# Graph layer and mixture of experts on one core: 36 weight chunks turned by transposing transfers instead of by the matrix engine

## The reference, cut to what matters

```
def gnn(x, C, A):                      # called with C = A = adj, 2048 x 2048
    S = (A + A.T) * 0.5 + eye          # degrees of S give dinv
    y = C @ (dinv[:, None] * S * dinv[None, :])
    return y @ x
def bit_quant(W):                      # per row of W
    scale = clip(mean(abs(W), -1), 1e-5, None)
    return clip(round(W / scale), -1, 1) * scale
def ffn(h):                            # 1 shared expert, 8 routed ones, top 1
    shared = silu(h @ sw1.T) @ sw2.T
    routed = gate * (silu(h @ ew1[e].T) @ ew2[e].T)   # e = best expert of the token
    return shared + routed
x = x + gnn(layernorm(x), adj, adj)    # x is 2048 x 512
x = x + ffn(layernorm(layernorm(x) * gamma + beta))
```

## Time and profile before

| | |
|---|---|
| median of three runs | 680.46 us (679.86 to 681.08) |
| profiled execution, first to last instruction (span) | 677.9 us |
| PE busy | 628.0 us, 93% |
| DVE, ACT, POOL busy | 69%, 55%, 26% |
| SP's transfer queue (q1) | 57.8% of 16 DMA engines, over the whole span |
| granted TensorE clock, mean | 0.997 |

### The profile page before, as it was taken

The page is one execution under the profiler, slowest core; times in us unless marked ns, Lnnn a source line. Parts: engine busy times, 40 slices in busy tenths (PEclk is TensorE's granted clock), DMA queues, the critical chain, the costliest instruction groups (busy, mean ns, idle before and its releaser), DMA issues.

```text
span 677.9 us, 15256 instructions
## 1 busy us (share of the span) xinstructions
PE 628.0 (93%) x4993; PEld 364.5 (54%) x4993; DVE 470.1 (69%) x1035; ACT 374.6 (55%) x692; POOL 178.2 (26%) x205
## 2 busy tenths in 40 slices
PE   0789899999987999999988999999999999999995
PEld 0334344444433444444434477776776777767772
DVE  4878997777775555678879399878865655555553
ACT  1667646668795777687746224566543333233331
POOL 2234443232210000003325244000122544353422
PEclk9999999999999999999999999999999999999998
DMA  8999980985768787767676967994395897777641
GB/s 348 418 421 414 421 335 2 221 208 158 227 198 293 258 281 270 266 225 237 210 256 233 226 181 179 232 232 127 73 191 153 191 195 184 184 173 196 168 137 32
DMA packets 107551, 151.67 MB, mean 224 GB/s; under 512 B 64734, under 2 KB 64734, under 8 KB 103392
## 3 DMA queue, kind: packets, MB, share of 16 engines
q1 hardware_dynamic: 91728, 117.74, 57.8%
q0 software_dynamic: 6960, 20.99, 10.3%
q10 hardware_dynamic: 8800, 12.09, 6.4%
HBM read 119.57 MB, written 19.16 MB: 205 GB/s over the span
## 4 chain that ended last, share of the span: by engine, by line
PE 56%; issue 28%; DVE 6%; DMA 6%; POOL 3%; ACT 0%; POOLq 0%; DVEq 0%; SPq 0%; ACTq 0%
PE bank L1625 20%; PE bank L1653 19%; DMA region<-in_adj_t 6%; PE bank L1502 5%; PE bank L1504 5%; PE bank L1503 5%; DVE region L1085 2%; DVE region L1081 1%; POOL rb L691 1%; POOL hb L698 1%; DVE region L1109 1%; DVE work L1105 1%; PE bank L1638 0%; DVE work L1340 0%; DVE work L1350 0%
## 5 line engine op out<-in xcount | busy, mean ns | idle before, releaser
L1653 PE MATMUL bank<-region,work 128*128 (+1 forms) x624 | 141.2, 379 | 1.9 <-DVE work L1350 1.9
L965 ACT ACTIVATE work<-work 128x512 f32<-128x512 f32 x78 | 48.5, 621 | 146.9 <-DVE work L1340 142.5
L1502 PE MATMUL bank<-zreg,work 128*128 (+1 forms) x256 | 97.2, 380 | 10.4 <-DVE work L1271 7.2
L1625 PE MATMUL bank<-zreg,region 128*128 128x128 f16 x1728 | 100.9, 219 | 0.0
L1625 PEld LDWEIGHTS bank<-zreg,region 128*128 (+1 forms) x1728 | 98.2, 98 | 4.5
L1502 PE MATMUL bank<-region,work 128*128 128x512 f16 x192 | 74.0, 385 | 25.7 <-DVE region L1109 25.5
L1504 PE MATMUL bank<-zreg,work 128*128 (+1 forms) x256 | 97.0, 379 | 0.0
L1503 PE MATMUL bank<-zreg,work 128*128 (+1 forms) x256 | 97.0, 379 | 0.0
L1653 PEld LDWEIGHTS bank<-region,work 128*128 128x128 f16 x624 | 59.1, 98 | 67.1 <-issue 4.4
L835 ACT ACTIVATE junk<-work 128x512 f16<-128x512 f32 x116 | 72.8, 627 | 24.6 <-DMA work<-in_w 18.3
L1350 DVE SCALAR_TENSOR_TENSOR work<-work 128x512 f16<-128x512 f32 x78 | 53.4, 691 | 38.8 <-ACT work L972 38.5
(11 more groups left out here) (163 smaller groups left out, 914.0 us busy)
## 6 DMA issues: line engine op xcount, KB each, us to landing
work<-in_w SPq DMA_DIRECT2D x58, 512.0 KB, 4.3
region<-in_adj SPq DMA_DIRECT2D x16, 1024.0 KB, 10.7
region<-in_adj_t SPq DMA_DIRECT2D x16, 1024.0 KB, 7.6
work<-in_adj_t SPq DMA_DIRECT2D x32, 384.0 KB, 4.4
zreg<-s_scratch SPq DMA_DIRECT2D x24, 256.0 KB, 4.0
xb<-in_w SPq DMA_DIRECT2D x10, 512.0 KB, 4.3
zreg<-in_x SPq DMA_DIRECT2D x4, 1024.0 KB, 9.8
h_scratch<-hb POOLq DMA_DIRECT2D x16, 256.0 KB, 4.3
```

The lines of the kernel that those rows point to most:

```text
L965: nc.scalar.activation(h1[:, cols], pre[:, cols], ACT.Silu).then_inc(h1_ok, 1)
L1502: nc.tensor.matmul(dst, a_hi, b_hi, start=start, stop=False, skip_group_check=True)
L1625: last = nc.tensor.matmul(ps_h[b][f // 4][:, (f % 4) * P:(f % 4 + 1) * P], w, ht[n % RING][:, c:c + P], start=(f % 4 == 0 and d == 0 and h ...
L1653: last = nc.tensor.matmul(ps_y[b][:, :].rearrange("p (d c) -> p d c", d=DB), h1hl[:, b, h, f * P:(f + 1) * P], w, start=(f == 0 and h == 0 ...
```

## The change

`by_dma` becomes true for every chunk but the eight early ones of even number that PE turns. SP gets `turn_later`, called two steps after the chunk's own step, right behind that step's `load_w`; PE's `turn_w` loses all its calls in the second product; ACT's `store_w` and DVE's `ternary` wait on `turned[...]` of the chunk's step instead of `tr_ok`. In macro 0 SP waits for the end of the first product (`z_acc`) before the first of these transfers, as their destination holds data of that product until then. Two loops are partly written out.

```
         def by_dma(q):
-            return isinstance(q, int) and (q >= LATE_FROM or q < ALL_BY_DMA or q < EARLY_CHUNKS and q % 2 == 1)
+            return not (isinstance(q, int) and ALL_BY_DMA <= q < EARLY_CHUNKS and q % 2 == 0)
...
+            def turn_later(g, m, s):
+                q, kind, c = later(g, m, s)
+                dst = (w1t if kind == 1 else w2t)[:, ds(c * CHUNK, CHUNK)]
+                sp.wait_ge(tern_ok, q + 1)
+                sp.dma_start(dst[:, WORDS:CHUNK].bitcast(I16).rearrange("p (k r) -> p k r", r=P),
+                             words16[:, s, :], transpose=True).then_inc(turned[s], 16)
...
                     if not weight_free(m):
                         load_w(later(g, m - (g == 2), s), s % 2)
+                    if s >= 2 and not weight_free(m):
+                        if isinstance(m, int) and m == 0 and s == 2:
+                            sp.wait_ge(z_acc, NT)
+                        turn_later(g, m - (g == 2), s - 2)
+                    elif s < 2 and not (isinstance(m, int) and (m == 0 or weight_free(m - 1))):
+                        turn_later(g, m - 1 - (g == 2 and m - 1 > IDLE), s + 2)
...
                 if by_dma(q):
-                    act.wait_ge(*turned_by(q))
+                    act.wait_ge(*turned_by(q, step))
                     nc.scalar.activation(values, dst[:, WORDS:CHUNK].bitcast(I8).rearrange("p (w b) -> p b w", b=2),
                                          ACT.Sign).then_inc(wt_ok, 1)
...
                     if by_dma(before_q):
-                        dve.wait_ge(*turned_by(before_q))
+                        dve.wait_ge(*turned_by(before_q, step))
...
                 for s in range(STEPS):
                     b = s % 2
-                    late_turn = first and g == 1 and s == 1
-                    idle = isinstance(m, int) and m == IDLE
-                    if s and not (late_turn or weight_free(m)):
-                        turn_w(later(g, m - (g == 2), s - 1), s - 1)
-                    elif s == 0 and isinstance(m, int) and m == 0:
-                        turn_w(early(ROUNDS - 1, early_count(ROUNDS - 1) - 1), 3)
-                    elif s == 0 and not (isinstance(m, int) and weight_free(m - 1)):
-                        turn_w(later(g, m - 1 - (g == 2 and not idle), STEPS - 1), STEPS - 1)
                     pe.wait_ge(atlo_ok, STEPS * m + s + 1)
```

More of the change, by code:

```diff
@@ L364, in by_dma, with turned_by @@
         def by_dma(q):
-            return isinstance(q, int) and (q >= LATE_FROM or q < ALL_BY_DMA or q < EARLY_CHUNKS and q % 2 == 1)
+            return not (isinstance(q, int) and ALL_BY_DMA <= q < EARLY_CHUNKS and q % 2 == 0)
         def nth_by_dma(q):
             return q if q < ALL_BY_DMA else ALL_BY_DMA + (q - ALL_BY_DMA) // 2
-        def turned_by(q):
-            if q < EARLY_CHUNKS:
+        def turned_by(q, step=None):
+            if isinstance(q, int) and q < EARLY_CHUNKS:
                 d = nth_by_dma(q)
                 return turned[d % 4], 16 * (d // 4) + 16
-            return late_turned[q % 2], 16 * ((q - LATE_FROM) // 2) + 16
+            if isinstance(q, int) and q >= LATE_FROM:
+                return late_turned[q % 2], 16 * ((q - LATE_FROM) // 2) + 16
+            s = q % STEPS if isinstance(q, int) else step
+            return turned[s], 16 // STEPS * (q - s - EARLY_CHUNKS) + 16 * (EARLY_BY_DMA // 4) + 16
         def weight_free(m):
@@ L386, in turn_count, with turn_bank @@
         def turn_count(q):
[L388 to L393, removed]
+            return (q - ALL_BY_DMA) // 2 + 1
+        def turn_bank(q):
+            return q // 2 % 2
         def later(g, m, s):
@@ L512, in load_shared @@
                 elif n >= 4:
-                    sp.wait_ge(tr_ok, LATE_FROM - EARLY_BY_DMA)
+                    for last in range(LATE_FROM - STEPS, LATE_FROM):
+                        sp.wait_ge(*turned_by(last))
                 else:
@@ L522, in load_routed @@
                 sp.dma_start(columns_of(n), hslot[n % SLOTS], transpose=True).then_inc(ht_in[n % RING], 16)
[L524 to L528, removed]
+            macro(0, 0, True)
+            with sp.Fori(1, 4) as m:
+                macro(0, m, False)
+            macro(1, 4, False)
+            macro(1, 5, False)
+            with sp.Fori(6, 8) as m:
+                macro(1, m, False)
             for m in range(IDLE, MACROS - 1):
@@ L836, in sums, with store_w @@
                                          accum_out=asum[:, b, a:a + 1]).then_inc(abs_ok, 1)
-            def store_w(chunk, b):
+            def store_w(chunk, step=None):
                 q, kind, c = chunk
@@ L848, in store_w @@
                 act.wait_ge(tr_ok, turn_count(q))
-                nc.scalar.activation(values, pst8[turn_bank(q, b)], ACT.Sign).then_inc(wt_ok, 1)
+                nc.scalar.activation(values, pst8[turn_bank(q)], ACT.Sign).then_inc(wt_ok, 1)
             act.wait_ge(dinvz_ok, 1)
@@ L862, in early_round @@
                     if q >= LAG:
-                        store_w(early(rnd, s - LAG) if s >= LAG else early(rnd - 1, s - LAG + early_count(rnd - 1)),
-                                (q - LAG) % 2)
+                        store_w(early(rnd, s - LAG) if s >= LAG else early(rnd - 1, s - LAG + early_count(rnd - 1)))
                     act.wait_ge(early_loaded[q % 3], 16 * (q // 3) + 16)
@@ L900, in macro @@
                         if not weight_free(m):
-                            store_w(later(g, mm, s - LAG), (s - LAG) % 2)
+                            store_w(later(g, mm, s - LAG), s - LAG)
                     elif first and s:
-                        store_w(early(ROUNDS - 1, s - LAG + early_count(ROUNDS - 1)), (s - LAG) % 2)
+                        store_w(early(ROUNDS - 1, s - LAG + early_count(ROUNDS - 1)))
                     elif not (first or isinstance(m, int) and weight_free(m - 1)):
-                        store_w(later(g, mm - 1, s - LAG + STEPS), (s - LAG) % 2)
+                        store_w(later(g, mm - 1, s - LAG + STEPS), s - LAG + STEPS)
                     if not weight_free(m):
@@ L936, in _ @@
             z_high(2)
-            store_w(early(ROUNDS - 1, early_count(ROUNDS - 1) - LAG), (EARLY_CHUNKS - LAG) % 2)
+            store_w(early(ROUNDS - 1, early_count(ROUNDS - 1) - LAG))
             macro(0, 0, True)
@@ L995, in late_weights @@
                     i = n - LATE_TILE - 3
-                    store_w(late(i), i % 2)
+                    store_w(late(i))
             def shared_tile(n, r):
@@ L1518, in _, with turn_w @@
             pe.wait_ge(consts, 7)
-            def turn_w(chunk, step):
+            def turn_w(chunk):
                 q, kind, c = chunk
@@ L1523, in turn_w @@
                     return
-                bank_ = turn_bank(q, step % 2)
-                slot = q % SLOTS_W if isinstance(q, int) else step
+                bank_, slot = turn_bank(q), q % SLOTS_W
                 pe.wait_ge(tern_ok, q + 1)
[L1527 to L1530, removed]
+                pe.wait_ge(wt_ok, q - 3)
                 for k in range(4):
@@ L1563, in early_round @@
                             chunk = (2 * EARLY + (EARLY + EARLY_W1) * (rnd - 2) - 1, 2, None)
-                        turn_w(chunk, k8 - 1)
+                        turn_w(chunk)
             early_round(1, 0, True)
@@ L1600, in macro @@
                     last.then_inc(p2_step, 1)
-                    if late_turn:
-                        turn_w(later(g, m, 0), 0)
             for g in range(2):
```

## The result

The changed kernel takes 696.79 us (median of 4 runs, 694.53 to 697.78) against 680.77 us for the kernel before (4 runs, 679.86 to 681.74): ratio 1.0224, 95% interval 1.0199 to 1.025. It is 12 to 16 us slower. The forecast was 2.4 us slower.

A forecast was written before the change was run, and what follows sets the result against it. PE sets the pace in macros 1 to 3, a loop over ACT and DVE in group 1, layer norm in group 2; 0 + 2.3 - 0.7 + 0.3 + 0.5 = +2.4 us gives 682.9 us, range 676.8 to 689.5.

The forecast's parts named there:

- Macro 0: Second product's first macro: earlier step starts cancelled by waits for ACT and `low`; taken as 0 us.
- Macros 1 to 3: Rest of group 0: DMA work of 17.2 us a macro against 16.44 now, so 2.3 us lost over three.
- first rival: Macros 1 to 3: the queue finds room, PE keeps its gain; 2.7 + 0.7 us won, 677.1 us; chance 0.25.
- The signs that I named: Macros 1 to 3: DMA share 0.95 or more, 3.88 us steps, longer `high` waits at macro starts, macros about 17 us.
- The price of a transposing transfer: On the DMA engines: 0.65 us alone, 1.21 us crowded, 0.80 us taken; the skill's rate gave 0.33 to 0.37 us.
- The third rival: Crowded price of 1.21 us everywhere: 8.3 us lost in macros 1 to 3, 2.0 in group 1; 690.8 us; chance 0.12.
- Group 1: Macros 4 to 7: 0.7 us gained from turns off the loop's path, 0.3 us charged for later loads.
- Group 2: Macros 9 and 10: load of step 40 behind a new transfer; 0.5 us lost, between 0 and 1.2 (one issue time).
- Moved waits of `store_w` and `ternary`: Second product: new waits for turned chunks are covered by three to four steps of slack; cost nothing.
- The part after 390 us: Feed-forward part after the second product: should keep its length; a change would mean a step left out.
- The 2.56 us around the span: Whole kernel: median of runs lies 2.56 us above the profiled span, added to 680.3 us to give 682.9 us.

The follow-up runs named there:

- e1: Changed kernel with only the 16 chunks of the first group (macros 0 to 3) turned by transfers, the other 20 by TensorE: 682.65 against 679.85 us.
- e8: Changed kernel with each turn in SP's queue moved behind the adjacency load of three steps later, ahead of the weight load: 685.63 against 680.36 us.
- e3: Changed kernel with only the four chunks of macro 9 turned by transfers, the rest by TensorE: 683.12 against 679.85 us.
- e5: Changed kernel with the 36 chunks not turned at all, neither by TensorE nor by transfer: 678.19 against 680.36 us.
- e15: The changed kernel run once more, unaltered, for a second profile: 691.22 against 679.48 us.
- e14: Changed kernel with all 36 turns behind the adjacency loads and each chunk turned twice by transfers: 697.2 against 679.88 us.
- e2: Changed kernel with only the 16 chunks of the second group (macros 4 to 7) turned by transfers, the rest by TensorE: 683.17 against 679.85 us.
- e4: Changed kernel with the 36 transfers made plain copies of the same 128 KB in the same queue positions, chunks left unturned: 686.53 against 679.85 us.
- e11: Changed kernel with turns behind the adjacency loads, by transfers for the first group's 16 chunks only, the other 20 by TensorE: 679.56 against 679.88 us.
- e12: Changed kernel with turns behind the adjacency loads, by transfers for the first and second groups' 32 chunks, macro 9 by TensorE: 682.6 us, ratio 1.004.
- e13: Changed kernel with turns behind the adjacency loads, by transfers for macro 9's four chunks only, the rest by TensorE: 681.3 us, ratio 1.0021.

## Why the prediction was wrong, point by point

- **Macro 0: 0 us.** Wrong. Step 4 comes 1.8 us later against step 3 in both profiles of after (from -0.3 at step 3 to +1.4 at step 4, from -0.9 to +0.9), 1.2 us in e1, and not in e8 (-1.2 to -1.6): the turns ahead of the loads. The half-clock step that follows can't be put down to the change, as e3 has it too.
- **Macros 1 to 3: 2.3 us, since the queue is full.** The step that the forecast rested on failed. It put 14.0 us of DMA work for the loads, 0.80 for a turn and a ceiling of 1.0 on the share: 17.2 us. Measured: the same loads take 0.84 x 15.54 = 13.1 us where PE doesn't turn (e5), a turn takes (1.01 - 0.84) x 15.54 / 4 = 0.66 us among them (e8), 15.7 in sum, and the macro takes 15.54. The share isn't a gauge with a stop either: it read 1.01 at 292 GB/s with PE busy throughout (e8), 1.12 at only 276 with PE idle 0.95 us (e15), and 1.15 at 316 (e14). Net of clock the three macros gain or lose about nothing (second profile, full clock there: +3.2 at step 5, +3.1 at step 16): PE's 0.22 us a step is won, as the first rival said, and given back at steps 12 and 16. That e1's loss (2.8 us) is near the 2.3 us forecast for this group is luck: in its profile it is all lost by step 5.
- **The signs that I named** came true in the main, and for another cause: the share above 0.95, matmul steps of 3.88 us, `high` waiting for loads at the first step of a macro, macros near 17 us (16.65 and 17.66). They can't tell a full queue from a wrongly ordered one; e8 does.
- **The price of a transposing transfer.** The Trainium skill (Advanced Engine Details and Errata, X-Bar Transpose) says that such a transfer is as fast as a plain one, 350 to 400 GB/s. The trace disagrees for these transfers: 131 KB in 0.66 us of all engines, by the share, is 199 GB/s. The rival that it led to had the macro that e8 reaches (15.5 us) with the wrong price.
- **The third rival.** Its 690.8 us lie near the 691.2 of e15, by luck: the 8.3 us that it put into macros 1 to 3 are not lost there, and group 1 is held by loads of the adjacency.
- **Group 1: -0.4 us.** Wrong in sign: +3.6 us alone (e2, step 16 to 31). I read steps 24 and 25 only the earlier trace rows, where idle time covers a late load, and took them for the whole loop; at step 27 `high` starts as its load lands, and there is no cover. The gain was overrated too: with no turning the group wins 0.5 us (e5, step 16 to 31).
- **Group 2: +0.5 us, at most one issue time.** I named the new wait in macro 10 and the loads of steps 41 and 42 behind it, but priced the issue alone. Behind them in the same program stand the loads of x, two transposing loads of h and `load_at` of step 44: 3.4 us in e3, of which 2.7 are its late issue.
- **Moved waits of `store_w` and `ternary`: nothing.** Right: PE's waits name `low` (27.1 of 30.4 us), not the stores, and no wait of ACT or DVE in the stage names a turned chunk.
- **The part after 390 us keeps its length.** Right in the second profile; the first has 3.6 us there that stay unexplained.
- **The 2.56 us around the span.** Too much by up to 1 us: where a run has both figures, 1.6 to 2.2 us lie between them (after 694.53 and 692.9). The profiled execution of before was a fast one, and the forecast's own sum would have given some 682 us.

The failures in macro 0, group 1 and group 2 are one: I asked how much work the transfer adds to the queue, and hardly what stands behind it in SP's order with no slack. The Trainium skill (DMA: Bandwidth & Descriptors, Two DMAs through the same engine are not ordered) says that descriptors within one queue of one DMA engine start in order. The rows of step 27 agree: an unchanged issue, a landing 1.2 us later.

## What to carry to other kernels

Before work is moved to a transfer queue, list for each place which load comes next in the issuing engine's program and whether its consumer starts the moment it lands; such a load can pay the issue, wait and data of what is put in front of it. Put the new transfer behind that load, waiting only for what has already happened. Here that took most of the loss away, but won nothing: the first group alone in this order takes 679.56 against 679.88 us. And test the gain first by leaving the work out: here it was about 2.2 us of 680, while each of the three groups lost about 3.

## What the runs showed of the hardware

- PE's granted clock fell from 1.00 to 0.50 (2.4 to 1.2 GHz) for 3.4 to 6.9 us after PE had been idle 2.1 to 5.2 us, ahead of steps 4, 12, 19 or 44 for instance. It stayed at 1.00 after like stalls: the kernel before at step 4 (3.17 us idle), e2 there (2.73), after at step 44 (3.46). An 18-matmul step then takes 5.2 us or more instead of 3.88 (step 4 of after 5.17, step 19 of e15 5.25, step 12 of after 5.58). A short stall can so cost twice.
- A transposing transfer of 128 KB held SP 1.19 us (median; up to 2.1 in after), a plain copy of the same bytes 0.50 us (e4).
- Two transposing loads of h from memory held SP 4.74 us before, 5.0 to 5.3 us in e5, e11 and e12 with no turn near them, and 5.3 to 6.0 us in e3, e13 and e15 behind turns: their issue isn't a fixed price. What sets it is not shown.
